# A mixture-of-experts and attention kernel on one core: rows of an expert tile turned by DMA transposes of fp16 halves instead of by TensorE

## The chip, the cores and the metric

One core of one Trainium2 chip runs the whole program in one launch. The metric is the device time of an execution in microseconds (us); lower is better.

## What is computed

x has 4 sequences of 2048 tokens of 256 numbers (8192 tokens). Its layer norm xn feeds two branches: attention with 16 heads of 16 and a distance penalty (ALiBi) per head, and a mixture of 8 experts of which each token takes 2, plus one shared expert. The result is x + attention * silu(experts). The reference, cut to what matters:

```python
xn = _layernorm(x, axis=-1)
# attention
qkv = (xn @ W_qkv.T + b_qkv)                       # q, k, v: 16 heads of 16
scores = einsum('bhqd,bhkd->bhqk', q, k) / sqrt(16) - slopes * |q - k|
s = (softmax(scores) @ v) @ W_out.T + b_out
# experts: two of eight for each token, by router scores
g = einsum('th,ehi->tei', xn, w_gate); u = einsum('th,ehi->tei', xn, w_up)
y = einsum('tei,eih->teh', silu(g) * u, w_down)
routed = einsum('teh,te->th', y, comb)             # comb: weights of the two chosen
shared = silu(xn @ sw_gate) * (xn @ sw_up) @ sw_down
return x + s * silu(routed + shared)
```

## The kernel before

The program has three stages, each a block with one instruction stream per engine. TensorE (PE), VectorE (DVE), ScalarE (ACT), GpSimd (POOL) and SyncE (SP) run their streams in order and wait on semaphores, so an instruction that waits holds everything behind it on its engine. Line numbers are those of the profile.

**Token stage (`tokens_stage`, 0 to about 280 us).** 16 blocks of 512 tokens. For block j, DVE computes the layer norm into `x[:, j % 2]` (fp32, 128 partitions x 4 x 256; `ln_stats` L870, `ln_apply` L883, the scaling at L890). PE turns it (L593), ACT and DVE split the turned block, times XS = 2**11, into a high and a low fp16 part (L751, L916), and all products are then made of fp16 parts: high by high, high by low, low by high (the list `PRODUCTS`). PE makes q and k (L599), v (L622), the router's logits (L631) and the shared expert (L640, L657). DVE reads q and k out (L901); ACT rounds each of the four pieces of 128 rows to fp16 (`split`, L731), POOL subtracts to get the low parts (L699), four times a block, and SP stores both parts (`store_parts`, L506; three DMAs for each piece, twelve a block: pieces 0 and 1 are k, pieces 2 and 3 are q) in `k_stack` and `q_stack`. `split` of a piece of the next block waits until the stores of this piece have landed (`parts_out`, L730). SP's order in block j is: stores of the k pieces, load of x for block j+4 (L493), store of the normalised rows of block j+2 in DRAM (`store_xn`, L525 to L527), stores of the q pieces, v (L512), shift (L514), and in some blocks expert weights (L521, L523) or the first attention loads (L1071, L1079). `xn` in DRAM holds one row of 256 fp32 numbers (1 KB) per token.

**Attention stage (`attend_stage`, about 280 to 1500 us).** 64 heads (4 sequences x 16), in an order in which heads with a narrow window (few columns, 8 to 10 chunks) and wide ones (up to 32 chunks and more) alternate. A head is cut into chunks of at most 1024 columns, 1306 in all. For chunk c, PE makes scores in one of three PSUM slots (`scores`, L1377), ACT takes the exponential (L1494), DVE multiplies the diagonal pieces (`fade`, L1519), and PE makes the weighted sum with V as the stationary operand (`weighted_sum`, L1403). PE runs `scores(c + 3)` before the weighted sum of chunk c, and it may do so when the exponential of chunk c has freed the slot (L1368).

The experts' work is laid between these chunks. 72 tiles of 256 routed token rows each pass through: POOL gathers the expert's weights (L1322, 128 x 768 fp32 words) and the rows (two gathers of 128 rows into `xs[:, i % 2, t]`, L1328); PE turns them by four transposes of 128 x 128 fp32 into the PSUM bank F (`turn_tile`, L1426 to L1434); DVE reads F twice and writes the high and the low fp16 part to `xT` (`take_tile`, L1537 to L1545); PE makes gate and up (`gate_up`, L1436, twelve matmuls of 256 columns), ACT the tanh (L1485), DVE the gated product (L1575, L1578), PE the down product (`down`, L1446), DVE the copy (L1585), and POOL scatters the result rows (L1334).

Where a part of a tile stands is decided by a table made at build time, not by the clock: FF_AT gives for each tile the chunk after which `turn`, `gate` and `down` are issued, each at least 2, 3 and 4 chunks after the one before (`FF_APART`), and a tile starts at least FF_EACH = 11300 score columns after the one before. POOL's gathers are paced in the same way: they wait for the exponential of a chunk that is so many columns past a part of tile i-2 (`PACE_W`, `PACE_XS`).

```python
def load_tile(i):                                   # POOL, L1317
    if i > 1:
        pool.wait_ge(ff_turned, i - 1)              # xs[i % 2] is free
    for t in range(2):
        if i > 1:
            pool.wait_ge(expd, after("turn", i - 2, PACE_XS[t]))
        nc.gpsimd.indirect_dma_start(xs[:, i % 2, t, :], None, keep["xn"], ...)
```

SP's stream in this stage goes head by head (L1275 to L1296). For head n: wait until the head before is read out, store it (L987, L988), load V of head n+2 (L1079), wait until all scores of head n are made, load K and Q of head n+3 (`load_head`, L1071), which uses the room of head n. Around some heads it also loads and stores sums and reciprocals.

**Output stage (`deliver_stage`, about 1500 us to the end).** The attention output is scaled, projected, multiplied with the gate and added to x. A second, general program behind a flag is not run with these inputs.

## Time and profile before

| | us |
|---|---|
| median of 3 runs | 1705.34 |
| lowest and highest of them | 1698.98, 1713.62 |
| the profiled execution: its span, first to last instruction | 1660.1 |
| median less that span (start and end of a launch, and the difference between executions) | 45.2 |
| busy in the span: PE | 1510.9 |
| ACT | 1317.2 |
| DVE | 1030.5 |
| POOL | 498.9 |

The span is one execution taken by the hardware profiler. Busy time is summed over all stages, and stages have different limits, so the share of an engine in the span says little by itself. For a stage one reads how much each engine is busy in it, what each waits for, and where a wait ends last. Idle time of an engine that isn't the bound costs nothing. A row of the timeline gives start, duration, engine, line, and in brackets the engine's idle time before it with what ended it; "SPq" rows are SyncE issuing DMAs.

### The profile page before, as it was taken

To read this page: it belongs to the slowest core of one execution; us is meant where nothing else is said; L and a number is where in the kernel's file an instruction comes from. 1 tells how busy PE (TensorE), PEld (TensorE's weight loads), DVE (VectorE), ACT (ScalarE), POOL (GpSimd) and SP (SyncE) were. 2 spreads that over 40 slices of the span, in tenths; PEclk is the share of its full clock that TensorE was granted. 3 is DMA by queue.
4 is the path that set the end of the run, shared out by engine and by line. 5 is a ranking of instruction groups with operands and counts; after the bars stand their busy time and mean duration, and the time that the engine had idled before them with its cause. 6 is when DMAs were issued, how large, how long until landed. Compare 5 with 4: busy or idle time off the path is not lost. (4 is left out here: it accounts for less than half of the span.)

```text
span 1660.1 us, 39707 instructions
## 1 busy us (share of the span) xinstructions
PE 1510.9 (91%) x15262; PEld 679.5 (41%) x15264; DVE 1030.5 (62%) x2745; ACT 1317.2 (79%) x1694; POOL 498.9 (30%) x477
## 2 busy tenths in 40 slices
PE   5998997889999999998999999989999999978985
PEld 3555564223334443343444333434444334323464
DVE  7787765988864454545544444454554444578697
ACT  5687776888898888887888888878888888888521
POOL 1232331000024333343343343333334343122143
PEclk9999999999999999999999999999999999999999
DMA  6858876343345455454454454454455554487884
GB/s 202 266 193 259 259 231 192 70 116 91 90 147 143 135 133 140 139 143 130 137 138 132 131 144 136 135 136 133 137 142 144 142 138 128 126 231 213 281 275 142
DMA packets 201089, 265.58 MB, mean 160 GB/s; under 512 B 90960, under 2 KB 158592, under 8 KB 200640
## 3 DMA queue, kind: packets, MB, share of 16 engines
q1 hardware_dynamic: 168256, 171.72, 37.0%
q0 software_dynamic: 24192, 82.86, 16.0%
q10 hardware_dynamic: 8448, 8.39, 1.4%
q8 instruction: 125, 2.05, 0.5%
q14 instruction: 68, 0.56, 0.1%
HBM read 180.56 MB, written 90.46 MB: 163 GB/s over the span
## 5 line engine op out<-in xcount | busy, mean ns | idle before, releaser
L1494 ACT ACTIVATE probs_att<-SC_att 128x1024 f32<-128x1024 f32 (+10 forms) x1306 | 1075.3, 912 | 159.5 <-PE SC_att L1377 151.8
L1403 PE MATMUL O_att<-probs_att,V_att 128*32 128x512 f32 (+7 forms) x8144 | 636.8, 409 | 44.3 <-DVE probs_att L1519 29.2
L1519 DVE TENSOR_TENSOR probs_att<-probs_att,decay 128x128 f32<-128x128 f32 x1024 | 265.1, 287 | 264.2 <-ACT probs_att L1494 259.1
L1403 PEld LDWEIGHTS O_att<-probs_att,V_att 128*32 128x32 f32 x8144 | 177.8, 110 | 200.9 <-issue 118.8
L1334 POOL DMA_INDIRECT ys<-ys_att,back_of_att x144 | 148.3, 1030 | 353.9 <-DVE ys_att L1585 249.4
L1377 PE MATMUL SC_att<-Q,K_turned_att 64*128 64x512 f16 (+7 forms) x1244 | 221.5, 310 | 14.1 <-ACT probs_att L1494 5.7
L1377 PE MATMUL SC_att<-Q,K 64*128 64x512 f16 (+9 forms) x1154 | 200.2, 300 | 6.2 <-DVE K_turned_att L1506 5.4
L1328 POOL DMA_INDIRECT x<-xn,row_of_att x144 | 140.1, 973 | 119.6 <-ACT probs_att L1494 108.0
L1377 PEld LDWEIGHTS SC_att<-Q,K_turned_att 64*128 64x128 f16 x1244 | 67.1, 94 | 263.3 <-ACT probs_att L1494 172.2
L1322 POOL DMA_INDIRECT x<-w_rows,owner x72 | 73.8, 1026 | 332.7 <-DVE row_of_att L1568 216.1
L699 POOL TENSOR_TENSOR inverse<-qk_tok,inverse 128x512 f16<-128x512 f32 x64 | 75.7, 1190 | 171.2 <-ACT inverse L731 164.2
L1443 PE MATMUL F_att<-x 128*128 128x256 f16 x864 | 109.2, 277 | 1.8 <-issue 1.5
L1377 PE MATMUL SC_att<-inverse,K_turned_att 64*128 64x512 f16 (+7 forms) x602 | 105.3, 307 | 3.9 <-issue 3.1
L1377 PEld LDWEIGHTS SC_att<-Q,K 64*128 64x128 f16 (+1 forms) x1154 | 65.7, 95 | 94.2 <-ACT probs_att L1494 59.7
L599 PE MATMUL GU_tok<-xT_tok,w_qkv_tok 128*128 128x512 f16 x384 | 90.5, 387 | 12.2 <-DVE xT_tok L916 12.2
L1525 DVE COPY out<-O_att 128x512 f32<-128x512 f32 x64 | 44.2, 691 | 91.7 <-PE O_att L1403 86.3
L1585 DVE COPY ys_att<-F_att 128x512 f32<-128x512 f32 x72 | 49.8, 692 | 80.0 <-PE F_att L1449 78.3
L1449 PE MATMUL F_att<-x 128*128 128x256 f32 x288 | 83.3, 412 | 16.9 <-DVE x L1578 16.8
L1377 PE MATMUL SC_att<-inverse 64*128 64x512 f16 (+8 forms) x560 | 95.6, 296 | 0.4 <-ACT probs_att L1494 0.4
L1443 PEld LDWEIGHTS F_att<-x 128*128 128x128 f16 x864 | 79.7, 99 | 25.4 <-issue 15.5
L1542 DVE TENSOR_SCALAR x<-F_att 128x512 f16<-128x512 f32 x72 | 49.7, 690 | 59.0 <-PE F_att L1433 55.6
L1377 PEld LDWEIGHTS SC_att<-inverse,K_turned_att 64*128 64x128 f16 x602 | 32.3, 93 | 119.7 <-ACT probs_att L1494 67.3
(203 smaller groups left out, 1674.4 us busy)
## 6 DMA issues: line engine op xcount, KB each, us to landing
K<-k_stack SPq DMA_DIRECT2D x86, 256.0 KB
Q<-q_stack SPq DMA_DIRECT2D x86, 256.0 KB
x<-ys POOLq DMA_DIRECT2D x32, 512.0 KB, 4.7
x<-in_x SPq DMA_DIRECT2D x24, 512.0 KB, 6.4
k_stack<-inverse SPq DMA_DIRECT2D x96, 128.0 KB
q_stack<-inverse SPq DMA_DIRECT2D x96, 128.0 KB
inverse<-k_stack SPq DMA_DIRECT2D x42, 256.0 KB
inverse<-q_stack SPq DMA_DIRECT2D x42, 256.0 KB
```

What stands on the lines that cost most here:

```text
L599: mm = pe.matmul(GU[:, m, :], w_qkv[:, w, c, m * P:(m + 1) * P], xT[:, j % 2, x, c, :], start=(k == 0), stop=(k == len(PRODUCTS) - 1))
L699: nc.gpsimd.tensor_tensor(parts[:, k, 1, :], qk[:, m, :], parts[:, k, 0, :], ALU.subtract).then_inc(part2, 1)
L1322: nc.gpsimd.indirect_dma_start(w[:, i % 3, :], None, keep["w_rows"], index(keep["owner"][:, i:i + 1])).then_inc(w_in[i % 3], 16)
L1328: nc.gpsimd.indirect_dma_start(xs[:, i % 2, t, :], None, keep["xn"], index(row_of[:, t, i:i + 1])).then_inc(xs_in[i % 2], 16)
L1334: nc.gpsimd.indirect_dma_start(keep["ys"], index(back_of[:, t, i:i + 1]), ys[:, i % 2, t, :], None).then_inc(ys_out[i % 2], 16)
L1377: mm = pe.matmul(SC[:, c % SLOTS, at:at + x1 - x0], (K_turned[at_turned] if side else K[at_k])[rows, k * P:(k + 1) * P], Q[at_k][rows, x0: ...
L1403: mm = pe.matmul(O[VW * g:VW * (g + 1), col:col + width * len(mine)], V[par][:, k, :], spans[:, j0:j0 + BPB * (len(mine) - 1) + 1:BPB, :], ...
L1443: mm = pe.matmul(F[:, n * TILE_IN:(n + 1) * TILE_IN], w_of(i, wp, c, n), xT[:, xp, c, :], start=(k == 0), stop=(k == len(PRODUCTS) - 1))
L1449: mm = pe.matmul(F[:, t * D:(t + 1) * D], hid[:, t * P:(t + 1) * P], w[:, i % 3, WGU:WROW], start=True, stop=True)
L1494: nc.scalar.activation(probs[home][:, side + chunk.base:side + chunk.base + chunk.width], SC[:, c % SLOTS, start:start + chunk.width], ACT ...
L1519: v.tensor_tensor(diag, diag, decay[:, head_of(chunk.head), :], ALU.mult).then_inc(faded, 1)
L1585: v.tensor_copy(ys[:, i % 2].rearrange("p t d -> p (t d)"), F[:]).then_inc(ff_y, 1)
```

## The change

The rows are split into fp16 halves before they are stored, and are turned by DMA in place of TensorE.

- In the token stage std is divided by XS (the scale of the square root at L724), so that x already holds the normalised rows times XS; the scales at L751 and L916 go. POOL makes of each block a high half (a cast, 128 x 1024) and a low half (a subtraction, 128 x 1024) in a new function `split_rows`: blocks 0 and 1 first, block j+2 after the four subtractions of block j. The two halves lie side by side, and `xn` in DRAM has rows of 512 fp16 numbers, 1 KB as before. `store_xn` waits for POOL's result (`pair_ready`) where it waited for DVE's. DVE's next write to x waits for POOL in place of the store.
- In the attention stage `turn_tile` (PE) and `take_tile` (DVE) go. SP gets `turn_tiles`: for each tile two DMA transposes of 128 x 512 fp16, from `xs[:, i % 2, t]` to `xT[i % 2]`, which now has two buffers (the second in the room of `w_o`). They stand in SP's stream of the head in which chunk TURN_AT[i] falls, between the load of V and the wait for the head's scores. A transpose waits for the gather of the rows (`xs_in`) and for the gate and up product of tile i-2 (`ff_gu`), not for a chunk.
- `gate_up` waits for both transposes (`xT_in`, 32 per tile) and for F to be read out (`ff_y`).
- A tile now starts with its gate. TILES_AFTER goes from 16 to 18, so tile 0's gate stays near its old place. Over the 72 tiles the gate comes 2 chunks earlier in 49 cases, at the same place in 15, and 1, 3 or 4 chunks earlier in 8.

```diff
-PREFIX_TURNS, LIST_TURN, LISTED_AFTER, TILES_AFTER = (31, 36), 61, 136, 16
-FF_APART = (("turn", 2), ("gate", 3), ("down", 4))
+PREFIX_TURNS, LIST_TURN, LISTED_AFTER, TILES_AFTER = (31, 36), 61, 136, 18
+FF_APART = (("gate", 3), ("down", 4))
+TURN_AFTER = 9500
...
                 def store_xn(j):
-                    sp.wait_ge(xn_ready, j + 1)
-                    sp.dma_start(block_rows(keep["xn"], j), x[:, j % 2]).then_inc(xn_stored[j % 2], 16)
+                    sp.wait_ge(pair_ready, j + 1)
+                    sp.dma_start(block_rows(keep["xn"], j), pair[:, j % 2].rearrange("p t s d -> p t (s d)")).then_inc(xn_stored[j % 2], 16)
...
+                def split_rows(j):
+                    pool.wait_ge(xn_ready, j + 1)
+                    if j > 1:
+                        pool.wait_ge(xn_stored[j % 2], 16 * (j // 2))
+                    high, low = pair[:, j % 2, :, 0, :], pair[:, j % 2, :, 1, :]
+                    nc.gpsimd.tensor_copy(high, x[:, j % 2]).then_inc(pair_high, 1)
+                    pool.wait_ge(pair_high, j + 1)
+                    nc.gpsimd.tensor_tensor(low, x[:, j % 2], high, ALU.subtract).then_inc(pair_ready, 1)
...
+                    if j + 2 < NBLK:
+                        split_rows(j + 2)
...
-                        dve.wait_ge(xn_stored[j % 2], 16 * (j // 2))
+                        dve.wait_ge(pair_ready, j - 1)
...
+    TURN_AT = [ORDER_AT + 4 * (i + 1) if i < 2 else after("gate", i - 2, PACE_XS[1] + TURN_AFTER) for i in range(TILES_IN)]
...
+                def turn_tiles(first, end):
+                    for i in range(TILES_IN):
+                        if not first <= TURN_AT[i] < end:
+                            continue
+                        sp.wait_ge(xs_in[i % 2], 32 * (i // 2 + 1))
+                        if i > 1:
+                            sp.wait_ge(ff_gu, 2 * (i - 1))
+                        for t in range(2):
+                            sp.dma_start_transpose(xT[i % 2][:, :, t * P:(t + 1) * P], xs[:, i % 2, t, :]).then_inc(xT_in[i % 2], 16)
...
+                    turn_tiles(FIRST_CHUNK[n], FIRST_CHUNK[n + 1])
                     if n + STACKS < BH:
                         sp.wait_ge(scored, FIRST_CHUNK[n + 1])
                         load_head(sp, keep, n + STACKS)
...
                     if i > 1:
-                        pool.wait_ge(ff_turned, i - 1)
+                        pool.wait_ge(xT_in[i % 2], 32 * (i // 2))
...
-                def turn_tile(i):
-                    pe.wait_ge(xs_in[i % 2], 32 * (i // 2 + 1))
-                    if i > 0:
-                        pe.wait_ge(ff_y, i)
-                    for c in range(DC):
-                        for t in range(2):
-                            at = c * TILE_IN + t * P
-                            mm = pe.transpose(F[:, at:at + P], xs[:, i % 2, t, c * P:(c + 1) * P], ident[:])
-                    mm.then_inc(ff_turned, 1)
...
                 def gate_up(i, n):
                     if n == 0:
                         pe.wait_ge(w_in[i % 3], 16 * (i // 3 + 1))
-                        pe.wait_ge(xT_ready, i + 1)
+                        pe.wait_ge(xT_in[i % 2], 32 * (i // 2 + 1))
                         if i > 0:
-                            pe.wait_ge(ff_hid, i)
+                            pe.wait_ge(ff_y, i)
...
-                def take_tile(i):
-                    dve.wait_ge(ff_turned, i + 1)
-                    if i > 0:
-                        dve.wait_ge(ff_gu, 2 * i)
-                    flat = xT[:, 0].rearrange("p c n -> p (c n)")
-                    v.tensor_scalar(flat, F[:], XS, None, ALU.mult).then_inc(xT_high, 1)
...
-            "xn": scratch("xn", (B * S, D), F32),
+            "xn": scratch("xn", (B * S, 2 * D), F16),
```

PE at the first tile, before. F is the experts' PSUM bank, SC the score slots, O the weighted sum; `F_att<-ident,x` is the turn, `F_att<-x` with x12 is gate and up.

```order
L1403 MATMUL O_att<-probs_att,V_att 32x512 x4
L1377 MATMUL SC_att<-inverse 128x512 x2
L1433 MATMUL F_att<-ident,x 128x128 x4
L1377 MATMUL SC_att<-inverse,K_turned_att 128x512 x2
L1403 MATMUL O_att<-probs_att,V_att 32x448 x3
L1403 MATMUL O_att<-probs_att,V_att 32x384
L1377 MATMUL SC_att<-inverse 128x512 x2
L1377 MATMUL SC_att<-inverse,K_turned_att 128x512 x2
```

The same place on PE after the change:

```order
L1434 MATMUL O_att<-probs_att,V_att 32x512 x4
L1408 MATMUL SC_att<-inverse 128x512 x2
L1408 MATMUL SC_att<-inverse,K_turned_att 128x512 x2
L1434 MATMUL O_att<-probs_att,V_att 32x448 x3
L1434 MATMUL O_att<-probs_att,V_att 32x384
L1408 MATMUL SC_att<-inverse 128x512 x2
L1408 MATMUL SC_att<-inverse,K_turned_att 128x512 x2
```

The four transposes are gone from between two chunks, and nothing takes their place on PE.

SP around two heads in the middle of the attention stage, after the change. `weighted` and `sums` are the stores of a head, V_raw, K, Q and inverse (the third room for K and Q) the loads for later heads; `w_o` and `x` as targets of DMA_TRANSPOSE are the two buffers of xT. Before the change the same rows stood there without the DMA_TRANSPOSE rows.

```order
L1004 DMA weighted<-out 128x1x64 x4
L1005 DMA sums<-out 4x8x64
L1011 DMA turned<-recip_parts 128x256 x3
L1096 DMA V_raw<-values 128x4x64
L1287 DMA_TRANSPOSE w_o<-x 128x4x128 x2
L1287 DMA_TRANSPOSE x<-x 128x4x128 x2
L1287 DMA_TRANSPOSE w_o<-x 128x4x128 x2
L1088 DMA inverse<-k_stack 64x2048 x2
L1088 DMA inverse<-q_stack 64x2048 x2
L1004 DMA weighted<-out 128x1x64 x4
```

A wide head takes the transposes of three tiles, and they stand behind the stores of the head before and ahead of the next K and Q loads.

POOL in the token stage after the change, from the start of the blocks. `inverse<-qk_tok,inverse` is the old subtraction (L699 before), `o<-x_tok` the new work, since the halves lie in the room called o.

```order
L700 CAST o<-x_tok 128x4x256
L702 TENSOR_TENSOR o<-x_tok,o 128x4x256
L714 TENSOR_TENSOR inverse<-qk_tok,inverse 128x512 x4
L700 CAST o<-x_tok 128x4x256
L702 TENSOR_TENSOR o<-x_tok,o 128x4x256
L714 TENSOR_TENSOR inverse<-qk_tok,inverse 128x512 x4
```

Two operations over 1024 columns stand behind each block's four over 512, and SP's store of `xn`, which stands ahead of the q stores in SP's stream as before, now waits for them.

## Rows read from the trace of the kernel before

**Rows 1.** The page: busy time, and PE and ACT in 40 slices.
```profile
PE 1510.9 (91%) x15262; PEld 679.5 (41%) x15264; DVE 1030.5 (62%) x2745; ACT 1317.2 (79%) x1694; POOL 498.9 (30%) x477
```

**Rows 2.** Busy us by stage: span, PE, PEld, DVE, ACT, POOL, clock, DMA share, GB/s.
```profile
0.00:280.00 280.00, 239.49 (x1731) 144.78 (x1731) 206.48 (x443) 201.72 (x304) 76.67 (x70) 0.99 0.72 230
480.00:1430.00 950.00, 907.21 (x9992) 384.74 (x9990) 475.24 (x1304) 808.97 (x1019) 360.31 (x358) 0.99 0.50 139
```

**Rows 3.** Waits of 480 to 1430 us: total, times, longest.
```profile
ACT probs_att L1494 <- PE SC_att L1377: 110.6, 209, 4.9
```

**Rows 4.** Groups of 480 to 1430 us: count | busy, mean ns | idle before.
```profile
L1403 PE MATMUL O_att<-probs_att,V_att 128*32 128x64 f32 (+7 forms) x5968 | 458.3, 406 | 17.3 <-DVE probs_att L1519 11.4 <-issue 5.1 <-ACT probs_att L1494 0.2
L1433 PE MATMUL F_att<-ident,x 128*128 128x128 f32 x288 | 47.2, 287 | 0.0
L1542 DVE TENSOR_SCALAR x<-F_att 128x512 f16<-128x512 f32 x72 | 49.7, 690 | 59.0 <-PE F_att L1433 55.6 <-issue 2.3 <-DVE recip L1037 1.0
L1544 DVE SCALAR_TENSOR_TENSOR x<-F_att,x 128x512 f16<-128x512 f32 x72 | 49.8, 691 | 2.5
```

**Rows 5.** Timeline of PE, SP around the turn of tile 68 (head 55).
```profile
1382.42 0.66 PE L1433 MATMUL F_att<-ident,x 128*128 128x128 f32 x4
1383.01 0.39 PE L1377 MATMUL SC_att<-Q,K_turned_att 64*128 64x512 f16 x2
1383.64 0.45 SPq L1079 DMA_DIRECT2D V_raw<-values  x1
1384.33 0.39 PE L1377 MATMUL SC_att<-Q,K 64*128 64x512 f16 x2
```

**Rows 6.** The same for tile 19 (head 23).
```profile
733.70 0.44 SPq L1079 DMA_DIRECT2D V_raw<-values  x1
739.91 0.39 PE L1377 MATMUL SC_att<-inverse 64*128 64x512 f16 x2
```

**Rows 7.** DMA issues of the page: count, KB each, median us to landing.
```profile
sums_in<-sums SPq DMA_DIRECT2D x4, 128.0 KB, 2.7
w_rows<-w_d_tok SPq DMA_DIRECT2D x8, 128.0 KB, 4.2
xn<-x_tok SPq DMA_DIRECT2D x16, 512.0 KB, 6.4
```

**Rows 8.** Timeline of the token stage, blocks 12 and 13: POOL and SP.
```profile
218.07 2.46 POOL L699 TENSOR_TENSOR inverse<-qk_tok,inverse 128x512 f16<-128x512 f32 x2 [7.71 <-ACT inverse L731]
223.48 1.17 POOL L699 TENSOR_TENSOR inverse<-qk_tok,inverse 128x512 f16<-128x512 f32 x1 [1.36 <-ACT inverse L731]
225.11 0.48 SPq L527 DMA_DIRECT2D xn<-x_tok  x1
232.36 2.46 POOL L699 TENSOR_TENSOR inverse<-qk_tok,inverse 128x512 f16<-128x512 f32 x2 [7.70 <-ACT inverse L731]
```

**Rows 9.** Timeline of blocks 8 and 9: SP's q stores, ACT's splits behind them.
```profile
169.66 5.33 SPq L506 DMA_DIRECT2D q_stack<-inverse  x6
178.28 0.62 ACT L731 CAST inverse<-qk_tok 128x512 f16<-128x512 f32 x1 [2.22 <-DMA q_stack<-inverse]
180.33 0.62 ACT L731 CAST inverse<-qk_tok 128x512 f16<-128x512 f32 x1 [0.47 <-DMA q_stack<-inverse]
```

**Rows 10.** Groups of the whole span: POOL's operations.
```profile
L699 POOL TENSOR_TENSOR inverse<-qk_tok,inverse 128x512 f16<-128x512 f32 x64 | 75.7, 1190 | 171.2 <-ACT inverse L731 164.2 <-issue 6.9
L1872 POOL TENSOR_TENSOR y_del<-y_del,x 128x1024 f32<-128x1024 f32 x8 | 18.8, 2347 | 52.8 <-DVE y_del L1929 52.8
```

**Rows 11.** Timeline: DVE's L890 without POOL beside it, and with it.
```profile
8.43 1.38 DVE L890 TENSOR_SCALAR x_tok<-x,mv_tok,rstd_tok 128x256 f32<-128x256 f32 x4
231.57 2.23 DVE L890 TENSOR_SCALAR x_tok<-x,mv_tok,rstd_tok 128x256 f32<-128x256 f32 x4
```

42 lines of the change are left out of this document (21 added, 21 removed).

## The prediction

> **What bounds the kernel now.** I read the page first, then busy time by stage, then the waits and groups of the stage with the tiles, and last the timelines of PE, ACT, POOL and SP. PE is the busiest engine of the whole span [rows 1], but that is an average over stages. Of the 950 us that hold the 72 tiles, PE is busy 907.2 and ACT 809.0 [rows 2]. So PE is idle 43 us there and ACT 141 us, and 110.6 us of ACT's idle time ends with a score matmul of PE [rows 3]: ACT is mostly the one that waits. PE sets the pace of this stage, at its full clock (0.99). The token stage is different: in 280 us PE is busy 239.5, DVE 206.5 and ACT 201.7 [rows 2]. There a loop of waits matters. ACT's rounding of a q piece waits until the stores of the same piece of the block before have landed: in block 9 it starts at 178.28, 8.6 us after SP began to issue these stores at 169.66 [rows 9]. In blocks 10 to 14 the loop has a little room and a block takes 14.29 us (232.36 less 218.07 [rows 8]).
>
> **PE and DVE lose the turn.** One turn is four transposes that hold PE for 0.66 us, and the scores behind start 0.59 us after it does (1383.01 less 1382.42 [rows 5]); the group's busy time agrees, 47.2 us for 72 turns [rows 4]. So 72 x 0.59 = 42.5 us leave PE. The time comes back in full only where PE doesn't run into a wait for ACT before ACT would have run dry. PE is idle for 43 of 950 us, 4.5%, so it is rarely ahead; I take off 4 us and reckon with **-38 us**. Bounds: -42.5, and -20 if half of the turns fall where ACT is the slower one. DVE loses 0.69 + 0.69 us a tile, 99.5 us of 475 [rows 2, 4]. DVE isn't the bound; what it gives is in the wait of the weighted sums for the diagonal product, 11.4 us in all [rows 4]. I take **-2 us** of it; bounds 0 and -11.
>
> **What stands in its place: SP.** A tile needs two transposes of 128 KB each. No transpose by DMA is in the trace. The nearest rows are plain 128 KB transfers, which land 2.7 or 4.2 us after their issue [rows 7], and issuing one holds SP for about 0.45 to 0.6 us [rows 5]. The second of a pair is issued behind the first, so a pair needs at least 0.6 + 2.7 = 3.3 us from the moment SP is free. Upper bound from rows: two in a row at the 6.4 us of a 512 KB transfer with 1.6 us of issue, 8 us. I take 5 us, near the 4.2 us row.
>
> In most cases that is hidden. The transposes wait for no chunk, the rows have been gathered about 20 us ahead of the gate, and SP idles most of the stage. But SP is in order: in a head that has just begun it still stores the head before and loads V. For each tile I read from the timeline when SP is through with this load in the head where TURN_AT falls, and when PE reaches the gate's new place. The tightest is tile 68: SP is free at 1384.09 and PE gets there at 1384.7, 0.6 us later [rows 5]. Twelve of the 72 have less than 7 us: 0.6, 1.0, 2.2, 3.1, 3.7, 3.8, 4.3, 4.4, 4.8, 5.0, 5.8 and 6.2, the last being tile 19, 734.14 against 740.3 [rows 6]; the next is 7.2. With a pair of 5 us nine tiles are late by 17 us in sum; with 4 us it is 10, with 6 us 27, with 8 us 54 (seventeen tiles), with 10 us 99. PE is the bound, and behind the waiting gate stand the weighted sum and all scores to come; the three score slots let ACT go on for two chunks but don't give PE's time back. So the price is one to one: **+17 us**, bounds 7 and 54.
>
> POOL's gather of the rows of tile i+2 now waits for the transposes of tile i, not for PE's turn. In the late tiles this moves it by a few us, against some 20 us that the rows lie ready: nothing. K and Q loads behind the transposes are for three heads ahead: nothing. Gates that stand two chunks earlier change no sum of work: nothing.
>
> **The token stage: POOL's two new operations.** The old subtraction over 512 columns takes 1190 ns, the two-input operation over 1024 columns 2347 ns [rows 10]. The new subtraction is priced at 2.35 us. A cast by POOL isn't in the trace; I bound it by 0.6 and 2.35 us and take half of the two-input operation, 1.2 us. Together 3.6 us a block. POOL has the time for it: it is idle 7.7 us before a block's first subtraction [rows 8]. What counts is who waits. In block 12 the last subtraction ends at 224.65 and SP stores xn at 225.11 [rows 8]. With the split between, xn goes out at 228.3, and the q stores behind it on SP 3.2 us later than now. These are the stores for which ACT's splits of the next block wait, and behind these in ACT's stream stand v, the logits and the turned x that PE needs. The loop then reads: from the start of the third split to the end of the fourth 2.7 us (178.28 to 180.95 [rows 9]), POOL's last subtraction 1.2, the split of the rows 3.6, xn 0.6, q stores to landing 8.6: 16.7 us a block, against 14.29. Of the twelve blocks 2 to 13 four take 16.6 us or more already; eight at 14.0 to 14.4 us are lengthened by 2.4: 19 us. In block 0 the expert loads (behind xn on SP) move by 4 us too. Against this, the x load ahead of the q stores is then 3 us further off, and they should land sooner; I take off 6. Sum **+17 us**. Bounds: +3 (fast cast, stores landing in 6 us) and +38 (a cast as long as the subtraction, all twelve blocks lengthened).
>
> DVE and POOL disturb each other. DVE's four scalings at L890 take 1.38 us when POOL is quiet and 2.23 us beside its subtractions [rows 11]. The new operations fall after the fourth subtraction, where DVE has row statistics and reads PSUM; I put nothing down for it. The Trainium skill (SBUF — State Buffer, on the shared port pair) says that one of the two engines gets the pair for a whole instruction and the other is blocked fully. By this rule a scaling caught behind the new subtraction would lose up to 2.35 us in a block, an estimate of at most 14 x 2.35 = 33 us; the two timeline rows agree with the rule in kind, at 0.85 us lost.
>
> **Sum.** -38 - 2 + 17 + 17 = -6 us, against the span of 1660.1: 1654. The median of the runs shown, 1705.3, lies 45.2 above this span; what lies around it doesn't change. So 1705.3 - 6 = 1699 us. About 1% (17 us) is what a measurement of this kernel can tell from no change.
>
> **Rivals.**
> 1. *Everything new is hidden: clearly faster.* A pair of transposes lands in 3.5 us (7 us late in sum), and the q stores land soon enough (+3). -38 - 5 + 7 + 3 = -33: 1672. For it: 2.7 us for 128 KB, and SP and POOL have much idle time. Against it: splits that start at the very moment of the landing in block 9 [rows 9].
> 2. *Slower: the pair of transposes is slow.* Place: `gate_up` on PE, waiting for `xT_in`. Price: 54 us with 8 us a pair, 99 with 10. -40 + 17 + 54 = +31: 1736. It decides from about 7 us a pair on (39 us late, +16). For it: the halves go as short pieces, and each tile's pair queues behind whatever SP has sent. Against it: 128 KB rows at 2.7 and 4.2 us. The Trainium skill (VectorE: DVE Perf Modes, The three transpose paths) gives 1309 ns for a 128 x 128 transpose by DMA; a pair holds eight of these, and the estimate by this page, if they run one after the other, is 10.5 us a pair and about 1790 us. No row here shows it.
> 3. *Slower in the token stage.* Place: ACT's third and fourth split. The loop grows by the upper prices, +38, and the pair takes 6 us, +27: -40 + 65 = +25, 1730. For it: the loop is closed already in several blocks. Against it: POOL's idle time.
> 4. *PE's time isn't on the path.* If ACT sets the pace, the turns give back 20 us only: -20 + 34 = +14, 1719. Against it: ACT's 110.6 us of waiting for scores.
>
> **Chances.** The forecast 0.38 (its own range 1685 to 1717), rival 1 0.26, rival 2 0.18, rival 3 0.11, rival 4 0.07. Faster by over 1% is rival 1 and the low edge of the forecast: 0.30. Slower by over 1% is rivals 2 and 3 and a part of 4: 0.31. Within 1%: 0.39. The range that should hold 8 times in 10 reaches from rival 1 to rival 2: 1666 to 1740.
>
> **What would show it.** In the profile after: PE's L1433 gone and PE busy less by 42 to 47 us; DVE busy less by about 100. ACT's waiting for scores falls from 110.6 to about 90 if the turns counted. Waits of the gate matmuls for a DMA of SP, about nine, 17 us in sum, all in tiles whose TURN_AT lies just behind a head's start; a time to landing of some 4 us for a transpose. In the token stage the end moves from about 280 to 297 us, SP's L527 stands 3 us behind POOL's last subtraction, and ACT's L731 waits for q_stack in nearly every block. The forecast is wrong if the token stage keeps its length, if the gates wait in more than twenty tiles, or if ACT's idle time doesn't fall although PE has less to do.

## The result, and the profile after

The changed kernel takes **1728.5 us** (median of 4 runs, 1718.2 to 1731.2), the kernel before 1708.6 us beside it (4 runs, 1699.0 to 1713.6). The ratio is **1.012, 95% interval 1.008 to 1.015**: slower by 20 us. The forecast was 6 us less than before. A second measurement of the unchanged changed kernel (after_again, below) gives 1.010 [1.005, 1.014].

The page's busy line [rows 1] and its group of the weighted sums (count | busy, mean ns | idle before):

```profile
PE 1504.3 (87%) x14974; PEld 654.7 (38%) x14976; DVE 952.7 (55%) x2601; ACT 1311.6 (76%) x1694; POOL 549.7 (32%) x509
...
L1434 PE MATMUL O_att<-probs_att,V_att 128*32 128x512 f32 (+7 forms) x8144 | 656.4, 419 | 55.9 <-issue 21.4
```

Then the busy time by stage in the changed kernel: token stage, lists, the stage with the tiles (from the first exp that follows the lists to the same exp late in the program), mixing, end. Columns as in [rows 2].

```profile
0.00:288.00 288.00, 241.49 (x1709) 145.55 (x1711) 215.25 (x432) 199.71 (x299) 125.55 (x102) 0.97 0.69 222
502.80:1502.30 999.50, 890.33 (x9555) 356.72 (x9557) 381.12 (x1136) 795.77 (x1006) 353.95 (x353) 0.96 0.60 149
1502.30:1624.90 122.60, 106.89 (x1222) 35.00 (x1225) 90.89 (x260) 109.18 (x146) 27.05 (x34) 0.97 0.72 206
```

The profile shown of the kernel before can't be set against this one directly. Its execution had a span of 1660 us while its timed runs took 1705. So the kernel before was profiled once more (before_again), and its span is 1707.3. The same stages, cut at the same exps:

```profile
0.00:277.40 277.40, 238.14 (x1713) 144.00 (x1713) 203.76 (x432) 199.53 (x300) 76.34 (x70) 0.99 0.72 231
494.80:1478.10 983.30, 917.54 (x9844) 386.02 (x9848) 470.70 (x1280) 801.44 (x1008) 351.91 (x352) 0.98 0.48 130
1478.10:1602.60 124.50, 107.08 (x1222) 34.89 (x1222) 91.02 (x260) 108.97 (x146) 26.95 (x34) 0.97 0.71 203
```

Read the second row of each. In the stage with the tiles PE is busy 917.5 us before and 890.3 after: the turn did leave PE. But PE's idle time (length of the stretch less busy) goes from 983.3 - 917.5 = **65.8 us to 999.5 - 890.3 = 109.2 us**. What the turn gave, idle time took back and more. DVE has 89.6 us less to do, near the 99 reckoned. The token stage ends 10.6 us later. Mixing is unchanged. The granted clock is 0.96 and not 0.98; a row of free_transposes below shows it at half behind a pause.

By stage, the span grows by 10.6 us in the token stage and 16.2 in the stage with the tiles; the others together are 8 us shorter. The waits of the stage with the tiles, changed kernel first, then before_again (total, times, longest):

```profile
ACT probs_att L1513 <- PE SC_att L1408: 136.3, 193, 4.1
PE SC_att L1408 <- ACT probs_att L1513: 39.5, 52, 3.2
ACT probs_att L1513 <- remote: 24.4, 11, 3.9
PE F_att L1464 <- issue: 14.7, 10, 2.5
```

```profile
ACT probs_att L1494 <- PE SC_att L1377: 141.9, 217, 4.3
PE SC_att L1377 <- ACT probs_att L1494: 13.9, 19, 3.4
ACT probs_att L1494 <- remote: 8.5, 3, 3.2
```

ACT's waiting for scores [rows 3] hardly falls. What grows is PE's waiting for a score slot that ACT hasn't emptied (13.9 to 39.5 us) and ACT's pauses for which the view names no cause on the core ("remote", 8.5 to 24.4 us). New are the late gates, whose wait for a DMA is shown as "issue", ten times, 14.7 us in all. One of them, tile 9, in the timeline (start, duration, engine):

```profile
634.78 0.60 SPq L1096 DMA_DIRECT2D V_raw<-values  x1
635.48 2.57 SPq L1287 DMA_TRANSPOSE w_o<-x  x2
639.24 1.47 PE L1464 MATMUL F_att<-w_o,x 128*128 128x256 f16 x12 [2.18 <-issue]
```

SP loads V of a head that has just begun, then issues the pair in 2.57 us; the gate starts 3.8 us after SP was free, having waited 2.18 us.

### The profile page after: what moved, and what is told of

It reads as the page before. It is cut to its first block and busy times, and to the rows that moved or that the text cites. A ratio compares the mean times of both kernels' runs of the same rounds, so it can differ in the third digit from the quotient of the medians.

```text
span 1725.7 us, 39110 instructions
## 1 busy us (share of the span) xinstructions
PE 1504.3 (87%) x14974; PEld 654.7 (38%) x14976; DVE 952.7 (55%) x2601; ACT 1311.6 (76%) x1694; POOL 549.7 (32%) x509
## 5 line engine op out<-in xcount | busy, mean ns | idle before, releaser
L1434 PE MATMUL O_att<-probs_att,V_att 128*32 128x512 f32 (+7 forms) x8144 | 656.4, 419 | 55.9 <-issue 21.4
L1538 DVE TENSOR_TENSOR probs_att<-probs_att,decay 128x128 f32<-128x128 f32 x1024 | 268.8, 288 | 456.0 <-ACT probs_att L1513 396.1
L1434 PEld LDWEIGHTS O_att<-probs_att,V_att 128*32 128x32 f32 x8144 | 181.5, 112 | 220.0 <-issue 155.5
L1408 PE MATMUL SC_att<-Q,K_turned_att 64*128 64x512 f16 (+7 forms) x1244 | 225.0, 315 | 43.4 <-ACT probs_att L1513 30.5
L1408 PE MATMUL SC_att<-Q,K 64*128 64x512 f16 (+9 forms) x1154 | 206.4, 307 | 11.2 <-DVE K_turned_att L1525 7.4
L1544 DVE COPY out<-O_att 128x512 f32<-128x512 f32 x64 | 44.3, 692 | 115.3 <-PE O_att L1434 91.3
L1605 DVE SCALAR_TENSOR_TENSOR gate_all<-x,share,gate_all 128x256 f32<-128x256 f32 x128 | 61.5, 482 | 11.2 <-DMA x<-ys 8.8
L748 ACT CAST inverse<-qk_tok 128x512 f16<-128x512 f32 x64 | 38.2, 612 | 37.6 <-DMA q_stack<-inverse 20.2
L1855 ACT ACTIVATE gate_all<-gate_all 128x1024 f32<-128x1024 f32 x16 | 16.7, 1055 | 62.8 <-POOL y_del L1879 62.8
```

The source lines that it names most:

```text
L1408: mm = pe.matmul(SC[:, c % SLOTS, at:at + x1 - x0], (K_turned[at_turned] if side else K[at_k])[rows, k * P:(k + 1) * P], Q[at_k][rows, x0: ...
L1434: mm = pe.matmul(O[VW * g:VW * (g + 1), col:col + width * len(mine)], V[par][:, k, :], spans[:, j0:j0 + BPB * (len(mine) - 1) + 1:BPB, :], ...
L1538: v.tensor_tensor(diag, diag, decay[:, head_of(chunk.head), :], ALU.mult).then_inc(faded, 1)
L1605: v.scalar_tensor_tensor(out=acc, in0=pairs[:, j % PAIRS_AHEAD, n, k, :], scalar=keep["share"][:, n, t:t + 1], in1=acc, op0=ALU.mult, op1= ...
```

## The experiments

In all kernels named "no_turn" or "free", and in double_transposes and plain_copies, tiles 1 to 71 are computed from tile 0's rows, so that the rows need not be turned in time. PE's idle time is always worked out as above from the row shown: length less the first busy number. Ratios are to the kernel before, timed on the same chip.

### before_again, after_again: both kernels as they are

> The kernel before, unchanged, for a profile on the chip on which the next three run. The profile shown of it had a span of 1660 us, 45 us below the median of its timed runs (1705). Theory A (that profile was of an unusually quick execution, or another chip): this span comes near the timed runs, 1695 to 1710 us, with a granted clock near the 0.96 of the changed kernel's profile and an end of the token stage within 2 us of 278 us. Rival (the profile is the normal case, and the timed runs hold something around the span): span near 1660 again, clock 0.98.

> The changed kernel, unchanged, on the chip and in the session of the three above, so that it has a profile and a ratio beside theirs. Its first measurement gave 1.0118 [1.0083, 1.0154]; expected again within that interval. If it falls below 1.006, the loss depends on chip or session, and the steps found by differences of ratios must be read with that in mind.

Measured: before_again 1709.1, span 1707.3, clock 0.972; after_again 1718.6 us, 1.0096 [1.0050, 1.0143]. Theory A holds: the profile on which my prediction rested was of a quick execution, with 41 us of idle PE time in the stage (cut at the same exps) where before_again has 66. What differs between two executions of one program is counted under free_transposes. The loss of the change repeats. Its stage in after_again:

```profile
501.50:1491.70 990.20, 881.85 (x9558) 354.38 (x9560) 379.83 (x1136) 795.66 (x1008) 354.39 (x353) 0.97 0.62 151
```

Idle time is 108.3 us here too.

### no_turn: the turn's time alone

```diff
                         for i in ff_due("turn", c):
-                            turn_tile(i)
+                            if i == 0:
+                                turn_tile(i)
```
(the same for take_tile on DVE; the gate waits for ff_y as the turn did.)

> The kernel before without the turn: only tile 0's rows are turned by TensorE and taken by VectorE, and all later tiles use that tile's rows, so what is left out is 71 of 72 turns and takes; gathers, gates and stores stay. Theory A (the term of my forecast: the turn's time comes back in full, TensorE sets the pace): 38 to 42 us faster than before, 0.976. Theory B (the tile stage has as much room on TensorE as the turn takes, or the time goes to waits for ScalarE): 20 us or less, 0.988 or more.

Measured: 1677.7 us, 0.9843 [0.9777, 0.9909], that is 27 us faster (16 to 38).

```profile
491.80:1441.80 950.00, 872.30 (x9560) 355.96 (x9564) 380.96 (x1138) 792.14 (x1007) 355.36 (x352) 0.98 0.50 135
```

PE's busy time is down by 45.2 us, and idle time up from 65.8 to 77.7. Between the theories (38 and 20 us), and the interval holds both: by the middle value most of the turn comes back, and not all.

### halves_no_turn and split_added: the token stage alone

halves_no_turn is the changed kernel with tile 0's pair of transposes only:

```diff
-                        if not first <= TURN_AT[i] < end:
+                        if i > 0 or not first <= TURN_AT[i] < end:
...
-                        pe.wait_ge(xT_in[i % 2], 32 * (i // 2 + 1))
+                        pe.wait_ge(xT_in[0], 32)
```

> The changed kernel with one pair of transposes only, tile 0's; every tile's gate uses these rows, so 71 pairs of transposes and their waits are left out. Against no_turn it adds the token stage's part alone (GpSimd's two operations a block, xn stored as fp16 halves, in 1 KB rows as before). Theory A (forecast, token stage +17): 17 us slower than no_turn. Theory B (from the profile after, in which the first exp starts 10 us later): 10 us slower than no_turn. Theory C (TensorE in the tile stage hides nothing of it, and the halves' gathers cost nothing): the whole difference lies before the first exp.

split_added is the kernel before with split_rows on GpSimd as in the change, and

```diff
                 def store_xn(j):
-                    sp.wait_ge(xn_ready, j + 1)
+                    sp.wait_ge(pair_ready, j + 1)
```

> The kernel before with GpSimd's cast and subtraction added in every block, and the store of xn waiting for them; xn itself and everything after the token stage stay as before. Theory A (the token stage's part of the change costs 13 us, as between no_turn and halves_no_turn): 10 to 17 us slower than before, 1.006 to 1.010, with the first exp at 288 us. Rival (part of that step lies in the tile stage, in the gate's new place or the form of xn): 3 to 8 us slower.

Measured: halves_no_turn 1690.7 us, 0.9899 [0.9823, 0.9975], 10 us more than no_turn by the ratios (13 by the medians), with the row below; split_added 1719.0 us, 1.0059 [1.0020, 1.0099], 10 us slower than before (3 to 17), with the first exp at 292 us in its profile.

```profile
502.40:1465.10 962.70, 875.49 (x9558) 353.90 (x9560) 380.37 (x1136) 793.66 (x1007) 355.27 (x353) 0.98 0.50 136
```

Two ways to the same 10 us, Theory B of the first and A of the second, near its low end. I take this as the token stage's price, on the strength of split_added: the step from no_turn to halves_no_turn is 10 us with 17 us of uncertainty either way. In split_added DVE still waits for the store of xn and not for GpSimd alone, which may lengthen it more than the change does. PE idles 87.2 us against no_turn's 77.7, so a part of the step may lie in the stage with the tiles; the intervals don't settle it.

### free_transposes, double_transposes, plain_copies: transposes that nobody waits for

free_transposes:

```diff
+                            sp.wait_ge(xT_in[(i - 1) % 2], 32 * ((i - 1) // 2 + 1))
                         for t in range(2):
-                            sp.dma_start_transpose(xT[i % 2][:, :, t * P:(t + 1) * P], xs[:, i % 2, t, :]).then_inc(xT_in[i % 2], 16)
+                            sp.dma_start_transpose(xT[min(i, 1)][:, :, t * P:(t + 1) * P], xs[:, i % 2, t, :]).then_inc(xT_in[i % 2], 16)
```

> The changed kernel with all 144 transposes issued at their places, but tiles 1 to 71 write theirs into a buffer that nobody reads, and every gate uses tile 0's rows, so no gate waits for a transpose. Against halves_no_turn it adds the transposes in flight alone. Theory A (the price of the transposes is that gates wait for them, as I reckoned): within 4 us of halves_no_turn, and some 15 us faster than the changed kernel. Theory B (transposes in flight hold up the engines themselves: the profile after has far more waits of the kind issue and remote on PE, DVE and ACT, and PE idles more in the 7 us after a pair is issued): 20 to 35 us slower than halves_no_turn, and these waits stay in its profile.

Here the gates wait for tile 0's pair only, and SP waits in addition for the landing of the pair before. double_transposes issues each pair again when it has landed; plain_copies has for tiles 1 to 71

```diff
-                            sp.dma_start_transpose(xT[min(i, 1)][:, :, t * P:(t + 1) * P], xs[:, i % 2, t, :])
+                            sp.dma_start(xT[1][:, :, t * P:(t + 1) * P], xs[:, i % 2, t, :].rearrange("p (m n) -> p m n", n=P))
```

> free_transposes with each of the 71 idle pairs issued a second time as soon as the first has landed: 286 transposes in all, no gate waits for one. Left out, as there: tiles 1 to 71 are computed from tile 0's rows. Theory B (transposes in flight hold up the engines; the step from halves_no_turn to free_transposes was +19 us, by medians 1690.7 and 1709.5): another +15 to +20 us, a ratio to before near 1.015, and TensorE's time at half clock in the tile stage, 41 us in halves_no_turn and 58 in free_transposes, rises to some 75. Rival (that step is noise between executions, or a fixed cost): within 4 us of free_transposes, 1.004.

> free_transposes with a plain DMA of the same bytes (128 KB in pieces of 256 bytes, same source, destination, queue and place) for every transpose but tile 0's. Left out, as there: tiles 1 to 71 are computed from tile 0's rows. Theory C (any such traffic disturbs, by its bytes and small pieces): as free_transposes, 1.004. Theory D (the transposing itself does, or SP being held 1.27 us by each instead of some 0.5): 15 to 19 us faster, as halves_no_turn, 0.990.

Measured: free_transposes 1709.5 us, 1.0041 [1.0008, 1.0073]; double_transposes 1734.5, 1.0171 [1.0118, 1.0224]; plain_copies 1693.8, 0.9944 [0.9919, 0.9970]. Their stages, in this order:

```profile
501.20:1481.80 980.60, 882.25 (x9556) 354.81 (x9560) 381.09 (x1136) 794.13 (x1008) 354.58 (x353) 0.97 0.62 152
```

```profile
507.10:1509.20 1002.10, 890.55 (x9558) 359.98 (x9560) 381.96 (x1136) 793.69 (x1008) 352.29 (x353) 0.97 0.73 168
```

```profile
504.30:1469.30 965.00, 881.94 (x9558) 357.76 (x9560) 379.86 (x1136) 794.87 (x1007) 354.36 (x353) 0.97 0.59 155
```

Transposes in flight cost without a gate waiting for them: 0.9899 to 1.0041 is 24 us (10 to 38), doubling them another 22 us, and PE's idle time goes 87, 98, 112 us. TensorE's time at the lower clock, expected to rise to some 75 us with the doubling, is 69 (counted in the trace). Plain DMAs of the same bytes and pieces are 16 us cheaper than the transposes, and their 8 us over halves_no_turn are not clear of nothing. Theories B and D have it. Whether it is the turning itself or SP's 1.27 us of issuing per transpose, plain_copies changes both and does not tell.

What the pauses look like in free_transposes, ACT and POOL around 942 us, and the clock before and behind:

```profile
939.63 0.95 POOL L1362 DMA_INDIRECT x<-xn,row_of_att  x1 [0.30 <-issue]
940.88 1.19 POOL L1368 DMA_INDIRECT ys<-ys_att,back_of_att  x1 [0.30 <-issue]
942.38 0.99 POOL L1368 DMA_INDIRECT ys<-ys_att,back_of_att  x1 [0.30 <-issue]
944.50 2.28 ACT L1519 ACTIVATE probs_att<-SC_att 128x1024 f32<-128x1024 f32 x4 [3.37 <-remote]
945.58 0.23 PE L1414 MATMUL SC_att<-Q,K_turned_att 64*128 64x64 f16 x2 [3.38 <-ACT probs_att L1519]
```

```profile
940.00:942.00 2.00, 1.88 (x22) 0.44 (x14) 1.00 (x3) 1.14 (x2) 1.70 (x2) 1.00 0.90 179
942.00:945.50 3.50, 0.21 (x2) 0.00 (x0) 0.17 (x1) 1.00 (x2) 1.06 (x2) 0.93 0.44 123
945.50:952.00 6.50, 6.42 (x42) 1.66 (x43) 1.47 (x5) 4.83 (x9) 0.00 (x0) 0.51 0.01 3
```

ACT stands idle from 941.13 us on for 3.4 us although PE has ended score matmuls for it, PE fills the three slots and pauses too, and then works at a granted clock of 0.51, that is at 1.2 GHz, for the next 6.5 us. A pause so costs its own length and then some. It begins while GpSimd issues the third of four indirect DMAs in a row. That led to the next runs.

The trace's record of semaphores says more of such a pause than the views do. The score matmuls that end at 940.90, 941.22 and 942.21 us signal their ends at 944.48, 944.52 and 944.66, and ACT starts 0.02 us behind the first of these signals. So ACT isn't slow: the word from PE reaches it 3.6 us late. (PE's ends are modelled; the trace can't tell whether the matmuls ended later than it says or only their signals came late.) All "remote" waits of ACT in the changed kernel, eleven of eleven, end so, 1.5 us or more behind the recorded end. Signals of score matmuls that come over 0.3 us late, of those recorded from 500 to 1440 us:

```
before, the execution of 1660 us     1 of 916
before_again                       137 of 818
no_turn                            152 of 832
halves_no_turn                     160 of 836
free_transposes                    172 of 825
changed (after)                    157 of 801
free_scatter_later (below)          98 of 863
after_scatter_later (below)         97 of 849
before_scatter_later (below)       149 of 800
before_spaced (below)               87 of 833
all_three (below)                   92 of 877
```

The first two rows are one program: this is what the quick execution lacked. No signal of an exp on ACT or of a product on DVE is 0.3 us late in any of these traces. What holds PE's signals back stays open. Loading of instructions, which the trace has as packets of queues of its own, doesn't look like the cause: such packets stand in or just ahead of 15 of the 28 ACT pauses over 1.5 us in free_transposes and 6 of 20 in before_again, against 44% of all stretches as long. GpSimd is issuing an indirect DMA in 44% of the time between an end and its late signal in free_transposes, against 37% of all time: a weak link by itself.

### early_turns, free_early: the transposes' place

```diff
-TURN_AFTER = 9500
+TURN_AFTER = 4000
```
(in the changed kernel, and in free_transposes.)

> The changed kernel with TURN_AFTER 4000 for 9500: every pair of transposes is issued some 5 us sooner after the gate two tiles before, so that those that now fall just behind a head's start fall into the head before, where SP is idle. Correct rows in every tile. Theory A (late gates cost 13 to 19 us, by free_transposes against the changed kernel): 10 to 19 us faster than the changed kernel, ratio 1.001 to 1.006, and no gate waits over 0.5 us for a transpose. Rival (what the late gates cost is small, and the rest of the change costs): 1.010 or more although the waits go.

> free_transposes with TURN_AFTER 4000 for 9500: the same 144 transposes, no gate waits for one, but they are issued some 4 us earlier against the gates. Left out, as there: tiles 1 to 71 are computed from tile 0's rows. Theory E (what transposes in flight cost depends on the place: at 9500 they stand beside GpSimd's gathers and stores of rows, at 4000 in a stretch without them): 0.990 to 0.996, as plain_copies, 10 us or more below free_transposes (1.0041). Rival (they cost the same wherever they are, and early_turns gained from its gates alone): 1.002 or more; then early_turns (0.9956) would stay unexplained.

Measured: early_turns **1694.7 us, 0.9956 [0.9928, 0.9985]**, with every tile computed as in the changed kernel, and faster than before; in its trace two gates wait over 0.5 us, 3.5 us in sum (after_again: nine, 17.9 us). free_early 1708.3, 1.0020 [0.9995, 1.0046].

```profile
502.00:1466.50 964.50, 874.42 (x9558) 353.63 (x9560) 379.53 (x1136) 794.70 (x1007) 354.28 (x353) 0.98 0.63 155
```

One constant is worth 24 us against the changed kernel, with 14 us less of waiting. But for idle transposes the place does not matter: free_early is within the interval of free_transposes, so Theory E falls for the transposes' side. Why free_early is some 10 us slower than early_turns, which does more, I can't explain: they differ in the buffer written and in one more wait on SP, and ran on different chips, each beside the kernel before. It puts a limit on the 24 us above: early_turns has the same 144 transposes, gates that wait for them, and is 10 us over halves_no_turn (0.9899 to 0.9956), not 24.

### free_scatter_later, after_scatter_later, before_scatter_later: GpSimd's stores 3 us later

```diff
-PACE_W, PACE_XS, PACE_YS = 1500, (3300, 5100), (1500, 3300)
+PACE_W, PACE_XS, PACE_YS = 1500, (3300, 5100), (4700, 6500)
```
(in free_transposes, the changed kernel, and the kernel before.)

> free_transposes with the other side moved: GpSimd's two stores of a tile's results wait for 3200 more columns of exp, some 3 us, so that they leave the stretch of the transposes. Left out, as there: tiles 1 to 71 are computed from tile 0's rows. Theory E, and the stores are what the transposes collide with: 8 us or more below free_transposes, under 1.000. Rival (collision with the gathers, or none): within 5 us of 1.0041.

> The changed kernel with GpSimd's two stores of a tile's results 3200 columns later, the move that made free_scatter_later 50 us faster than free_transposes. Theory F: 35 to 50 us faster than the changed kernel, 0.980 to 0.990, late gates kept. Rival (it works only with tiles that don't wait for transposes): less than 20 us faster, above 1.000.

> The kernel before with the same move of the stores. Theory F in its narrow form (only four indirect DMAs in a row cost, and the kernel before has its gathers 5 us ahead of the stores): within 8 us of before, 0.995 to 1.005. Theory G (the old place of the stores costs in every version, with or without the change, and the change is only one more load on top): 25 us or more faster than before, under 0.985.

Measured: free_scatter_later 1656.8 us, **0.9724** [0.9689, 0.9759], 54 us below free_transposes by the ratios; after_scatter_later 1686.9, 0.9898 [0.9861, 0.9935], some 35 us below the changed kernel; before_scatter_later 1767.6, **1.0374** [1.0338, 1.0409], 64 us above before. The stages, in this order:

```profile
501.20:1427.20 926.00, 862.87 (x9556) 352.16 (x9557) 379.87 (x1136) 791.55 (x1007) 352.67 (x353) 0.99 0.65 161
```

```profile
501.80:1459.30 957.50, 868.11 (x9558) 354.18 (x9560) 379.04 (x1136) 794.62 (x1007) 353.10 (x353) 0.98 0.63 156
```

```profile
493.70:1545.30 1051.60, 945.08 (x9844) 394.00 (x9848) 471.94 (x1280) 796.67 (x1007) 349.88 (x352) 0.95 0.45 122
```

PE idles 63.1, 89.4 and 106.5 us. No theory foresaw the third. PE's waits for a score slot fall from 44.3 us in free_transposes to 11.3 in free_scatter_later (500 to 1440 us). The times of GpSimd's five indirect DMAs of a tile (the stores are those of the tile whose gate it is, the gathers those of the tile two later), as medians over the tiles, in us from the start of a gate (counted in the traces; gates are some 13 us apart):

```
kernel                weights  rows         stores        PE idle
before_again           -1.9    -0.3   1.1    6.7   8.3     66
changed (after)         1.7     4.0   5.4    6.9   8.6    109
free_transposes         1.8     4.4   5.7    7.1   8.6     98
free_scatter_later      1.8     4.0   5.5    9.6  11.1     63
before_scatter_later   -0.6     1.2   2.9   10.8  12.3    107
```

Here is what the prediction had not seen. The pacing of the gathers was counted from the turn and is now counted from the gate, and the gates come two chunks sooner. So the gathers moved 4 us towards the stores, which stayed where they were against the gate, and the changed kernel issues five indirect DMAs within 7 us. In before_scatter_later the stores run into the next tile's gathers in the same way (10.8, 12.3, then about 13.7 and on). ACT pauses over 1.5 us between 500 and 1440 us number 20 in before_again, 33 in the changed kernel, 28 in free_transposes, 13 in free_scatter_later and 56 in before_scatter_later; of the 28, 18 begin within 0.8 us of the issue of a store, of the 13 six, where a fifth to a quarter of all ACT instructions do. Not all of them are late signals: 23 of the 28 end with one that is over 0.3 us late, 33 of the 56 and 7 of the 13; the others wait for PE's work in the ordinary way. That the pauses and the place of the stores go together is shown; how an issue on GpSimd could hold back PE's signals is not. A kernel without transposes in flight was not run with its stores later (halves_no_turn, no_turn), so whether the stores collide with the transposes or cost by themselves is open.

### gathers_back, early_gathers_back, before_spaced: is it the spacing?

```diff
-PACE_W, PACE_XS, PACE_YS = 1500, (3300, 5100), (1500, 3300)
+PACE_W, PACE_XS, PACE_YS = -2500, (-1000, 800), (1500, 3300)
...
-TURN_AFTER = 9500
+TURN_AFTER = 13800
```
(early_gathers_back: TURN_AFTER 8300. before_spaced: the kernel before with 5200, (7600, 9400), (4700, 6500).)

> The changed kernel with GpSimd's gathers of a tile's weights and rows put back to where the kernel before has them against the gate: PACE_W -2500 and PACE_XS (-1000, 800), some 4 us sooner, and TURN_AFTER 13800, so that the transposes stay where they were. Theory F (by moving the pacing from the turn to the gate the change put the four indirect DMAs of a tile, which were 5 us apart in two pairs, into one row, and this costs in the tile stage): at least 12 us faster than the changed kernel, a ratio to before of 1.003 or less. Rival (their place is nothing, as I forecast): within 5 us of the changed kernel, 1.007 to 1.012.

> early_turns with the gathers put back as in gathers_back, and TURN_AFTER 8300 so that the transposes stay at early_turns' places. gathers_back alone changed nothing (1.0128), but its gates came 27 us late in sum, against 18 in the changed kernel. Theory H: with the late gates gone the wider spacing of gathers and stores shows, 8 us or more faster than early_turns (0.9956), 0.991 or less. Rival (only the stores' place counts, or the gathers now collide with the transposes): 0.994 or more.

> The kernel before, turn by TensorE and all, with GpSimd's five indirect DMAs of a tile where all_three has them against the gate: gathers some 4 us later (PACE_W 5200, PACE_XS (7600, 9400), counted from the turn) and stores some 3 us later (PACE_YS (4700, 6500)). Theory H (how these DMAs are spaced against each other sets how often ScalarE pauses, in either kernel; before_scatter_later was 3.7% slower because its stores ran into the next tile's gathers): 25 to 45 us faster than before, 0.974 to 0.985, and the rest of all_three's lead (0.9654), 15 us or more, is what the change itself is worth. Rival (the gain of the spacing exists only with the turn away from TensorE): within 10 us of before, over 0.994.

Measured: gathers_back 1723.1 us, 1.0128 [1.0095, 1.0161]; early_gathers_back 1691.4, 0.9955 [0.9934, 0.9976]; before_spaced 1698.2, 0.9982 [0.9959, 1.0004]. The last two stages:

```profile
500.80:1460.00 959.20, 874.61 (x9558) 355.56 (x9560) 381.12 (x1136) 791.38 (x1008) 356.25 (x353) 0.98 0.62 156
```

```profile
495.40:1470.80 975.40, 913.73 (x9844) 384.31 (x9848) 469.34 (x1280) 801.95 (x1007) 348.70 (x352) 0.98 0.48 131
```

Three misses, and the rivals took all three. Putting the gathers back gained nothing, with late gates (nine, 26.7 us in sum) or without (0.9955 against early_turns' 0.9956): with the stores at 7.2 and 8.5 us and the next tile's gathers at 11.4 to 14.5 (medians, as above) the five DMAs still lie within 8 us, as they do in the kernel before, and ACT's long pauses (28 as against 27 in early_turns) only move from the stores to the gathers of rows, 19 of the 28. before_spaced takes back the 64 us of before_scatter_later, yet gains nothing measurable on the kernel before: PE idles 61.7 us instead of 65.8, although fewer of its signals are late (87 of 833, against 137 of 818). So later stores gave 35 us and more where rows are turned by DMA and nothing in the kernel before. That PE's lighter load makes the difference is a guess, since no_turn was not run with its stores later. And how closely the five stand is no rule by itself: gathers_back and early_gathers_back changed it and gained nothing.

### late_early and all_three: the versions that beat both

late_early is early_turns with

```diff
-                    if j + 2 < NBLK:
-                        store_xn(j + 2)
                     if j == 0:
...
                     store_rest(j)
+                    if j + 2 < NBLK:
+                        store_xn(j + 2)
```

> early_turns, and in the token stage xn of block j+2 is stored after the q pieces and the rest of block j, not ahead of them. Correct rows in every tile. Theory A (the token stage's loss of 10 us, first exp at 288 against 278 us, is that the q stores wait behind xn for GpSimd's two operations): first exp back to 280 us or sooner, and 8 to 10 us faster than early_turns: 0.990. Rival (the loss is GpSimd's operations disturbing VectorE, or other waits of xn's ring): first exp stays at 286 or more, ratio as early_turns, 0.9956.

all_three adds PACE_YS = (4700, 6500).

> The changed kernel with TURN_AFTER 4000, xn stored behind the q pieces, and the stores of the tiles' results 3200 columns later. If the three are independent (late_early 0.9936, the stores another 35 to 50 us): 0.965 to 0.973, faster than every version so far. If they remove the same pauses: 0.975 to 0.985.

Measured: late_early 1695.5 us, 0.9936 [0.9909, 0.9963]; all_three **1643.5 us, 0.9654 [0.9627, 0.9680]**, 59 us faster than the kernel before and 75 to 79 us faster than the changed one by the ratios; it computes all that both do. Their stages:

```profile
495.10:1474.60 979.50, 883.71 (x9549) 357.26 (x9549) 380.57 (x1136) 794.52 (x1006) 352.72 (x352) 0.97 0.60 152
```

```profile
489.80:1419.70 929.90, 864.35 (x9558) 353.05 (x9560) 379.15 (x1136) 791.40 (x1007) 352.98 (x353) 0.98 0.65 161
```

In late_early the first exp is back at 278.8 us, 9 us sooner than in early_turns (287.9): the order on SP was the token stage's loss. Its ratio shows only a part of these 9 us, 0.2% with intervals of 0.3% on each. In all_three PE idles 65.6 us, as in the kernel before, and is busy for 53 us less (917.5 to 864.4, a part of it by the better clock); the effects add, as the first case expected, and more: the three steps alone (0.0140, 0.0020 and 0.0198 to 0.0220) would give 0.972 to 0.974. Against before_spaced (0.9982), in which GpSimd's DMAs stand nearly alike, all_three is 56 us faster.

## Why the prediction was wrong

Forecast -6 us; measured +20. The direction and the likeliest case were wrong; the range (1666 to 1740) held the time. Two terms failed: the transposes were priced by the waits of the gates alone, "one to one: +17 us", and cost 34 to 37; the turn was priced at 40 us with DVE's part, and gave 27. The token stage erred the other way, 10 for 17. By the measured terms the sum is -27 + 10 + 37 = +20. In ratios, the steps are before 1, no_turn 0.9843, halves_no_turn 0.9899, free_transposes 1.0041, changed kernel 1.0118 and 1.0096: -27, +10, +24 and +9 to +13 us. Each step has an uncertainty of 8 to 17 us.

- **"PE and DVE lose the turn", -38 and -2.** Mis-sized. PE's busy time fell as reckoned (45.2 us in no_turn, with 42 to 47 expected), but the turn alone is worth 27 us (16 to 38), with DVE's part in it. My "PE is idle for 43 of 950 us, so it is rarely ahead" was read from the profile with the 1660 us span; the usual one has 66, and taking the work away adds 12. The 45.2 us between span and median, which I took for what lies around a span, were the difference between two executions: before_again's span is 2 us below its time.
- **"What stands in its place: SP", +17.** This is the step that failed most, by "So the price is one to one". The waits themselves came, in kind and size: ten gates late by 14.7 us (nine by 17.9 in after_again) against nine by 17; of my twelve tight tiles 9, 12, 19, 22, 33, 37, 40, 61, 65 and 68 are those ten. A pair takes 3.8 us from SP's being free where I took 5. But the time lost by the pairs is 34 to 37 us (halves_no_turn 0.9899 to the changed kernel's 1.0096 and 1.0118), twice their waits. free_transposes has none of the waits and 24 us of the loss, and moving the transposes (early_turns) gave 24 us where 14 us of waiting went. What transposes do beside being waited for had no term in my sum.
- **"POOL's gather ... nothing. Gates that stand two chunks earlier change no sum of work: nothing."** The reason was incomplete. I had looked at who waits for the gathers and not at what they run beside, and they moved 4 us towards the stores. But as far as it was tested the "nothing" stands: gathers_back (1.0128) is no faster than the changed kernel, early_gathers_back (0.9955) is level with early_turns (0.9956). The stores hardly moved against the gate (6.7 and 8.3 us before, 6.9 and 8.6 after), so the 35 us of after_scatter_later are a gain that the changed kernel leaves lying, not a part of its loss.
- **"The token stage", +17.** 10 us. The two operations take 1.04 and 2.13 us, 3.2 us where I had 3.6:

```profile
L702 POOL TENSOR_TENSOR o<-x_tok,o 128x1024 f16<-128x1024 f32 x16 | 34.0, 2127 | 7.9 <-issue 6.7
L700 POOL CAST o<-x_tok 128x1024 f16<-128x1024 f32 x16 | 16.7, 1041 | 2.0 <-DVE x_tok L907 2.0
```

  The chain to SP was as I had it, 0.02 us behind POOL, [rows 8] answered by

```profile
219.45 2.13 POOL L702 TENSOR_TENSOR o<-x_tok,o 128x1024 f16<-128x1024 f32 x1
221.60 0.37 SPq L531 DMA_DIRECT2D xn<-o  x1
222.08 3.72 SPq L510 DMA_DIRECT2D q_stack<-inverse  x5
228.85 0.62 ACT L748 CAST inverse<-qk_tok 128x512 f16<-128x512 f32 x1 [1.32 <-DMA q_stack<-inverse]
```

  But the loop of 16.7 us a block is not there. The third split starts at 214.46, 228.85 and 243.54 us: 14.4 and 14.7 us a block, against 14.29 before. The stores are issued later and land sooner, 6.8 us after issue instead of 8.6 [rows 9]; the load of x stands 2.5 us ahead of them instead of 1.1, which may be why, but no run shows it. Half of the 10 us comes from block 0 alone, ACT's first split of block 1 starting at 45.10 us where it was 39.58: POOL's two operations (36.69 to 39.93 us) stand ahead of the expert loads and the q stores there. The rest is spread over the blocks.
- **The shared port.** Each of DVE's scalings takes 703 ns in the changed kernel and 649 in before_again, 64 x 54 ns = 3.5 us; in early_turns, with the same token stage, it takes 672 ns, and in late_early, with only SP's order changed, 642. My estimate by the rule of the Trainium skill (SBUF — State Buffer, the shared port pair), up to 33 us, supposed a collision in every block; these means show hardly any.
- **The rivals.** The sign was that of rivals 2, 3 and 4. Rival 2's price of the pair, 8 to 10 us, didn't come: 3.8 us from SP's being free. The Trainium skill (VectorE: DVE Perf Modes, The three transpose paths) gives 1309 ns for one transpose of 128 x 128; my estimate from it, eight one after the other in 10.5 us, doesn't agree with this trace. Rival 2's sum (1736) and rival 3's (1730) lie nearest to 1728.5, but by prices that didn't come: the pair was not slow, and the token stage cost 10 us, not 38. Rival 4 (1719) had one thing right: the turn gave 27 us, not all of its 42. None had a term for what the transposes cost beside their waits.

Open stays why PE's signals come late, and so why transposes that nobody waits for cost time. The traces show that in the versions with the change the late signals are fewer where the stores stand later, and the runs that moving the gathers doesn't help; no trace shows a wait for any of these DMAs.

## What to carry to other kernels

Work that leaves the busiest engine comes back only as far as the other engines' pauses allow: set the forecast against the idle time of a usual execution, and profile the kernel before more than once, since the profile read here hid 25 us of it. A span well under the median of the timed runs is the warning. When work goes from an engine to a DMA queue, the waits for it are only a part of its price: here they were half. Run the kernel once with the transfers left out and once with transfers that nobody waits for. When a change renames the point from which transfers are paced, write down for each where it stood and where it stands now, and try both places: here putting the gathers back gave nothing, and moving stores that the change had not touched gave 35 us. A constant that only places a DMA (TURN_AFTER, PACE_YS) is worth a run by itself before a change is judged.

## What the runs showed of the hardware

- Transposes by DMA cost time while no gate waits for them: 144 of 128 x 512 fp16, at the change's places, took 24 us of a kernel that is bound elsewhere (0.9899 to 1.0041), 142 more another 22 us (1.0171). Plain DMAs of the same bytes took 8 us (0.9944). Issued earlier, and waited for, the 144 took 10 us (early_turns, 0.9956).
- SP is held 1.26 us by each transpose (median in free_transposes), and 0.64 us by a plain DMA of the same bytes and pieces (plain_copies).
- PE's signals can reach ACT up to 4.8 us behind the recorded end of the matmul, several in one burst, while those of ACT and DVE never come 0.3 us late in these traces. How many do differs between executions of one program: 1 of 916 score signals in the execution of 1660 us, 137 of 818 in that of 1707 us.
- ACT pauses over 1.5 us mostly begin beside GpSimd's indirect DMAs: 24 of 26 in halves_no_turn within 0.8 us of such an issue, where half of all its instructions are. Most of them (20 of the 26) end with a late signal of PE.
- Behind a pause of PE of 3.4 us the granted clock was 0.51 for the next 6.5 us. Over the stage with the tiles it was 0.99 with 63 us idle (free_scatter_later) and 0.95 with 107 (before_scatter_later).
